# Statistics ahead of fused tile 0, one residual tile on VectorE, and a new order of tails and turnings in the middle passes of a hybrid layer

## What is computed

```python
x = x + attn(layernorm(x))        # itself normalised again, causal attention, plus its residual
x = x + ffn(layernorm(x))
x = x + s4d(layernorm(x))         # a long convolution over the first axis (here length 2), plus D * x
x = x + ffn(layernorm(x))

def ffn(x):                        # 256 -> 768 -> 256, weights rounded to fp8
    gate = silu((x @ fp8(gate_w)) * gate_scale)
    up   = (x @ fp8(up_w)) * up_scale
    return ((gate * up) @ fp8(down_w)) * down_scale
```

## Time and profile before

| what | value |
|---|---|
| median of 3 runs | 130.63 us (130.6 to 130.78) |
| the profiled execution | 130.82 us |
| its span, first to last instruction | 129.0 us |
| busy, share of the span: PE / DVE / POOL / ACT | 90% / 75% / 68% / 60% |
| granted TensorE clock | 1.000 |
| chain that ended last, by engine | PE 53%, DVE 26%, POOL 9%, issue 5%, DMA 2%, ACT 2% |
| pass 0 / 1 / 2 / 3 starts at | 54.6 / 71.94 / 89.53 / 107.83 us |

### The profile page before, as it was taken

One profiled execution on the slowest core, in us unless ns is written; L12 is line 12 of the kernel. 1 busy time (PEld: TensorE's weight loads), 2 busy tenths in 40 slices (PEclk: granted clock), 3 DMA queues, 4 the chain that ended last, 5 costly groups with the idle time before them and its releaser, 6 DMA issues.

```text
span 129.0 us, 2086 instructions
## 1 busy us (share of the span) xinstructions
PE 116.4 (90%) x666; PEld 77.1 (60%) x666; DVE 96.1 (75%) x224; ACT 77.3 (60%) x146; POOL 87.9 (68%) x172
## 2 busy tenths in 40 slices
PE   5997979977999999999999999989999879999930
PEld 5885548536767858746559545557446456455720
DVE  0499999999965587758675899947899944956471
ACT  2235368627966466957955368865578774486700
POOL 2256899999999888983333578889978860049631
PEclk9999999999999999999999999999999999999999
DMA  3999900000000000000000000000000000002204
GB/s 95 304 315 365 329 28 3 5 0 0 0 3 0 3 5 0 0 0 0 0 0 5 0 0 0 0 3 5 0 0 3 0 0 5 0 0 81 81 0 163
DMA packets 5666, 5.80 MB, mean 45 GB/s; under 512 B 1124, under 2 KB 5144, under 8 KB 5656
## 3 DMA queue, kind: packets, MB, share of 16 engines
q1 hardware_dynamic: 4776, 5.65, 13.1%
q10 hardware_dynamic: 816, 0.02, 0.4%
q0 software_dynamic: 64, 0.02, 0.1%
HBM read 4.63 MB, written 1.05 MB: 44 GB/s over the span
## 4 chain that ended last, share of the span: by engine, by line
PE 53%; DVE 26%; POOL 9%; issue 5%; DMA 2%; ACT 2%; POOLq 0%; DVEq 0%; ACTq 0%
PE psum L1170 21%; PE psum L1185 11%; PE psum L1109 7%; PE psum L1084 5%; POOL rstd L283 4%; DVE stats L680 4%; DVE down_raw L769 3%; DVE grid L760 3%; PE psum L1049 3%; PE psum L1131 2%; DMA x_in<-in_x 2%; DVE grid L761 2%; PE psum L1097 2%; POOL f_tail L439 2%; ACT h_rows L547 2%
## 5 line engine op out<-in xcount | busy, mean ns | idle before, releaser
L439 POOL TENSOR_TENSOR f_tail<-fused,f_head 128x512 f16<-128x512 f32 x12 | 14.3, 1189 | 15.7 <-ACT f_head L600 15.6
L595 ACT ACTIVATE gated<-psum,scales 128x512 f32<-128x512 f32 x24 | 16.4, 682 | 13.4 <-PE psum L1170 13.3
L1185 PE MATMUL psum<-down,f_head 128*128 128x256 bf16 x96 | 22.0, 273 | 0.5 <-POOL f_tail L439 0.5
L932 DVE SCALAR_TENSOR_TENSOR fused<-psum,up_scales_fit,gated 128x512 f32<-128x512 f32 x24 | 17.6, 738 | 5.9 <-PE psum L1170 3.6
L1185 PE MATMUL psum<-down,f_tail 128*128 128x256 bf16 x96 | 22.0, 272 | 0.0
L600 ACT ACTIVATE f_head<-fused 128x512 f16<-128x512 f32 x24 | 14.9, 621 | 2.5 <-DVE fused L932 2.4
L939 DVE TENSOR_TENSOR f_tail<-fused,f_head 128x512 f16<-128x512 f32 x12 | 8.7, 727 | 10.3 <-ACT f_head L600 10.3
L283 POOL TENSOR_TENSOR rstd<-var_eps,neg_half 128x2 f32<-128x2 f32 x16 | 13.1, 820 | 2.4
L1170 PE MATMUL psum<-h_head,up 128*128 128x512 f16 x48 | 14.3, 379 | 0.0
L1170 PE MATMUL psum<-h_tail,up 128*128 128x512 f16 x48 | 14.3, 379 | 0.0
L1170 PE MATMUL psum<-h_tail,gate 128*128 128x512 f16 x48 | 14.3, 379 | 0.0
(11 more groups left out here) (167 smaller groups left out, 260.0 us busy)
## 6 DMA issues: line engine op xcount, KB each, us to landing
x_in<-in_x SPq DMA_DIRECT2D x4, 256.0 KB, 4.5
out<-x_in SPq DMA_DIRECT2D x4, 256.0 KB, 2.1
qkv_sb<-in_qkv SPq DMA_DIRECT2D x3, 256.0 KB, 4.3
gate_raw<-in_gate_w SPq DMA_DIRECT2D x1, 768.0 KB, 6.4
up_raw<-in_up_w SPq DMA_DIRECT2D x1, 768.0 KB, 8.2
down_raw<-in_down_w SPq DMA_DIRECT2D x1, 768.0 KB, 9.9
wo_sb<-in_o_proj SPq DMA_DIRECT2D x1, 256.0 KB, 5.3
down_scale_all<-in_down_scale SPq DMA_DIRECT2D x1, 128.0 KB, 9.8
```

The lines of the kernel that those rows point to most:

```text
L439: pool.tensor_tensor(f_tail[:, m, :], fused[:, m % FUSED, :], f_head[:, m, :], ALU.subtract).then_inc(f_tail_by_pool, 1)
L595: act.activation(gated[:, m % 2, :], psum[:, BANK_GATE[m % 2], :], ACT.Silu, scale=gate_scales[:, m:m + 1]).then_inc(gated_ready, 1)
L932: dve.scalar_tensor_tensor(out=fused[:, m % FUSED, :], in0=psum[:, BANK_UP[m % 2], :], scalar=up_scales_fit[:, m:m + 1], in1=gated[:, m % ...
L1185: last = pe.matmul(column(BANK_DOWN[t // 2], H * (t % 2), H), part[:, m, t * P:t * P + P], down16[:, m, :], start=(m == 0 and t % 2 == 0 a ...
```

## The change

Six edits, all by hand in the engines' programs; the number of instructions on VectorE and GpSimd shifts by one each middle pass.

- VectorE: the last residual tile of the batch (x2 of tile 3 of 4) is added on VectorE (add_x1) instead of GpSimd, with its own semaphore; statistics of the first pair come before fuse(n, 0), those of the second pair after it; tail 0 stands between fuse 1 and fuse 2; tail 4 replaces tail 3 and stands behind fuse 5.
- GpSimd: three residual tiles instead of four; tails 1, 2, 3 in middle passes instead of 1, 2, 4, all in front of the last inversion; the shift is written ahead of the std product.
- ScalarE: the first pair of z rows stands before head 1.
- TensorE: on tile 0 of every pass the order is gate heads, up heads, gate tails, up tails; turn_h(n+1, 1) comes after down 4 instead of before it.

```diff
-        POOL_TAILS = [(1, 3, 4), (1, 2, 4), (1, 2, 4), (1, 3, 4)]
+        POOL_TAILS = [(1, 3, 4), (1, 2, 3), (1, 2, 3), (1, 3, 4)]
...
                 pool.wait_ge(rstd_ready[n], k + count)
+                pool.tensor_tensor(neg_mean_rstd[:, n, k:k + count], mean_rstd[:, n, k:k + count],
+                                   rstd[:, n, k:k + count], ALU.mult).then_inc(shift_ready[n], count)
                 if with_std:
                     pool.tensor_tensor(std[:, k:k + count], var_eps[:, n, k:k + count], rstd[:, n, k:k + count],
                                        ALU.mult).then_inc(std_ready, count)
-                pool.tensor_tensor(neg_mean_rstd[:, n, k:k + count], mean_rstd[:, n, k:k + count],
-                                   rstd[:, n, k:k + count], ALU.mult).then_inc(shift_ready[n], count)
...
-                    residual(0, x2, x1, range(first, first + T), x2_ready)
+                    residual(0, x2, x1, range(first, first + T - 1), x2_by_pool)
                     inverse_std(2, first, 2, negative_mean=True, with_std=True)
                     inverse_std(2, first + 2, 2, negative_mean=True, with_std=True)
                     tail(n, POOL_TAILS[n][0])
+                    tail(n, POOL_TAILS[n][1])
                     inverse_std(3, first, 2, negative_mean=True)
-                    tail(n, POOL_TAILS[n][1])
+                    tail(n, POOL_TAILS[n][2])
                     inverse_std(3, first + 2, 2, negative_mean=True)
-                    tail(n, POOL_TAILS[n][2])
...
                 gate(n, 2)
+                if n in (1, 2):
+                    z_rows(tiles[0])
+                    z_rows(tiles[1])
                 head(n, 1)
...
-                if n in (1, 2):
-                    z_rows(tiles[0])
-                    z_rows(tiles[1])
...
-                dve.wait_ge(x2_ready, tiles[-1] + 1)
+                b, t = tile_of[tiles[-1]]
+                dve.wait_ge(x2_by_pool, (T - 1) * b + min(t + 1, T - 1))
+                if t == T - 1:
+                    dve.wait_ge(x2_by_dve, b + 1)
                 tile_stats(2, tiles, x2)
+
+            def add_x1(k):
+
+                dve.wait_ge(down_read, k + 1)
+                dve.tensor_tensor(x2[:, k, :], scaled_down[:, k, :], x1[:, k, :], ALU.add).then_inc(x2_by_dve, 1)
...
+                    add_x1(tiles[-1])
+                    x2_stats(first)
                     fuse(n, 0)
-                    x2_stats(first)
                     x2_stats(second)
                     fuse(n, 1)
+                    tail(n, 0)
                     fuse(n, 2)
-                    tail(n, 0)
...
                     fuse(n, 4)
-                    tail(n, 3)
                     fuse(n, 5)
+                    tail(n, 4)
                     tail(n, 5)
...
             def gate_up(n, m):
-                for w, banks, made, read in ((gate16, BANK_GATE, gate_made, gated_ready), (up16, BANK_UP, up_made, fused_ready)):
+                if m == 0:
+                    for w, banks, made, read in BOTH:
+                        gate_up_part(n, m, w, banks, h_head, h_head_ready)
+                    for w, banks, made, read in BOTH:
+                        gate_up_part(n, m, w, banks, h_tail, h_tail_ready).then_inc(made, 1)
+                    return
...
                 turn_h(n + 1, 0)
                 down(n, M - 3)
+                down(n, M - 2)
                 turn_h(n + 1, 1)
-                down(n, M - 2)
                 down(n, M - 1)
```

More of the change, by code:

```diff
@@ L182, in hybrid_layer @@
         down_made, down_read = sem("down_made"), sem("down_read")
-        x2_ready, x3_ready, lag_ready, x4_by_pool, x4_by_dve = sem("x2_ready"), sem("x3_ready"), sem("lag_ready"), sem("x4_by_pool"), sem("x4_by_dve")
+        x2_by_pool, x2_by_dve, x3_ready, lag_ready, x4_by_pool, x4_by_dve = sem("x2_by_pool"), sem("x2_by_dve"), sem("x3_ready"), sem("lag_ready"), sem("x4_by_pool"), sem("x4_by_dve")
         tanh_in, tanh_out, trig_in, trig_out, magnitude_ready, taps_ready = sem("tanh_in"), sem("tanh_out"), sem("trig_in"), sem("trig_out"), sem("magnitude_ready"), sem("taps_ready")
-        POOL_TAILS = [(1, 3, 4), (1, 2, 4), (1, 2, 4), (1, 3, 4)]
+        POOL_TAILS = [(1, 3, 4), (1, 2, 3), (1, 2, 3), (1, 3, 4)]
         DVE_TAILS = [tuple(m for m in range(M) if m not in tiles) for tiles in POOL_TAILS]
@@ L1160, in _, with gate_up_part @@
             pe.wait_ge(gate_up_ready, 2)
-            def gate_up(n, m):
-                for w, banks, made, read in ((gate16, BANK_GATE, gate_made, gated_ready), (up16, BANK_UP, up_made, fused_ready)):
+            BOTH = ((gate16, BANK_GATE, gate_made, gated_ready), (up16, BANK_UP, up_made, fused_ready))
+            def gate_up_part(n, m, w, banks, part, ready):
+                for c in range(C):
+                    if m == 0 and w is gate16:
+                        pe.wait_ge(ready, n * C + (c + 1))
+                    last = pe.matmul(column(banks[m % 2], 0, S), w[:, c, m * P:m * P + P], part[:, c, :],
+                                     start=(part is h_head and c == 0), stop=(part is h_tail and c == C - 1))
+                return last
+            def gate_up(n, m):
+                if m == 0:
[4 more added lines that the diff above has]
+                    return
+                for w, banks, made, read in BOTH:
                     if m >= 2:
                         pe.wait_ge(read, n * M + (m - 1))
[L1166 to L1172, removed]
+                    gate_up_part(n, m, w, banks, h_head, h_head_ready)
+                    gate_up_part(n, m, w, banks, h_tail, h_tail_ready).then_inc(made, 1)
             def down(n, m):
```

## The result

The changed kernel takes 133.88 us (median of 4 runs, 133.8 to 133.9) against 130.7 us beside it (130.6 to 131.06): a ratio of 1.0237, 95% interval 1.0216 to 1.0257. It is slower by 3.2 us. The profiled execution took 133.9 us.

A forecast was written before the change was run, and what follows sets the result against it. GpSimd's closed chain was taken to set the middle passes, with TensorE 90% busy. Passes + 1.72 and + 0.24 us, last pass and start + 0.1, together + 2.1 on the median 130.63: 132.7; range 131.2 to 134.3.

The forecast's parts named there:

- the sum: Pass 1 + 1.72 us, pass 2 + 0.24, last pass and start + 0.1; together + 2.1, giving 132.7.
- S: Start of GpSimd's first inversion after its pass starts: 4.17 us in pass 1, 3.40 in pass 2; before, 3.78.
- The addition: VectorE's new residual addition ahead of the statistics: 0.38 us plus 0.22 for running beside a GpSimd addition.
- the rule of the Trainium skill: VectorE instructions with two SBUF inputs and GpSimd instructions reading SBUF exclude each other; the sum would be 0.2 to 0.4 longer.
- the row at 116.90: A VectorE tail before the change, 0.91 us where an undisturbed one took 0.69; source of the 0.22 disturbance.
- The chain: GpSimd from first inversion to end of last shift in a middle pass: 11.84 us, before 10.40 in pass 1.
- From the shift to the next pass: End of GpSimd's last shift to the next pass's start: 3.30 us instead of 3.41, through the moved turning.
- Idle time before up tile 2: TensorE in pass 1 waits 0.5 us more for fused tile 0, at no cost because the turning waits for GpSimd.
- Last pass: Last pass and start get 0 to 0.2 us longer, taken as 0.1.
- A sign that did not come: TensorE would be idle before the second turning for over 1 us in each middle pass.
- tail 4 in place of tail 3: On VectorE behind gated 5, it ends before the turning can start: cost 0.
- rival 1: ScalarE's late heads delay GpSimd's chain: 1.2 us of waits over both passes, with pass 2's old disturbances 134.0; chance 0.10.

The follow-up runs named there:

- e3: Kernel before with only the tails changed: GpSimd makes tails 1, 2, 3, all ahead of the last inversion, VectorE makes tail 4; ratio 1.0205.
- e4: Changed kernel with the second turning ahead of down tile 4 again; ratio 1.0173 to the kernel before.
- e5: Kernel before with only the first pair's statistics put ahead of fused tile 0 in both middle passes; ratio 1.0077.
- e10: Changed kernel with VectorE's fused tile 2 behind the first pair's convolution in pass 2; ratio 1.0207 to the kernel before.
- e7: Changed kernel with tails and second turning as before, and in pass 2 VectorE's fused tile 2 behind the first pair's convolution; ratio 0.9990 to the kernel before.

## Why the prediction was right, and where its size was off

The direction and the mechanism were right: slower, by GpSimd's third tail ahead of the last inversion, with 133.88 us inside the range of 131.2 to 134.3. The most likely value, 132.7, was 1.2 us low: the sum had + 1.72 and + 0.24 for the two passes, and they measured + 2.34 and + 0.80. Step by step:

- **S**, the first inversion after the start of its pass: forecast 4.17 and 3.40, measured 76.06 - 71.89 = 4.17 and 95.22 - 91.82 = 3.40. The 0.87 by which the late turning moves VectorE's beginning, the 0.67 won by fused tile 0, and the early scaled_down of pass 2 were right. The addition took 0.75 where I had 0.60. That fits VectorE waiting for GpSimd's second residual tile to end and GpSimd's third then waiting for the addition (it took 0.91 where the others took 0.73), as the rule of the Trainium skill that I had weighed has it, and not as the row at 116.90 had it; S did not suffer, because the addition started 0.06 sooner than I had it (74.27) and the statistics start a little ahead of the end that the record gives it.
- **The chain**: forecast 11.84, measured 12.22 and 12.38. This is the term that failed most, 0.38 and 0.54. The third tail (1.24) is as forecast, and e3, which has it alone, has a chain longer by 1.48 and 1.28. Mis-sized were the two inversions of norm 2 (80.39 - 76.06 = 4.33 and 99.55 - 95.22 = 4.33, forecast 4.03), because mean_rstd and the shift, and no longer the power, now fall beside VectorE's operations with two SBUF operands (0.60 and 0.46 where they take 0.20 alone): + 0.30 in each pass. From tail 1's start to tail 2's it took 1.62 in both passes (forecast 1.45), with a wait for head 2 of 0.46 in pass 1, and one of 0.28 behind a tail of 1.34 in pass 2: + 0.17. One more tail beside VectorE's operations took 1.33 (82.01) and 1.34 (104.14) instead of 1.16, and was 0.17 and 0.24 longer up to the next operation. Against this the first inversion of norm 3 took 1.67 and 1.73 up to its tail, where I had 1.89.
- **From the shift to the next pass**: forecast 3.30, measured 91.82 - 88.28 = 3.54 and 110.92 - 107.60 = 3.32. In pass 1 VectorE's tail 5 took 0.93 instead of 0.69, beside GpSimd's lag products, and down tile 5, which the moved turning had put right behind it, waited 0.83. Before, the same tail beside the same products took 0.69, so it is a matter of how the two fall together.
- **Idle time before up tile 2**: forecast 0.5 under GpSimd's. The record has 0.24 of idle time, but the start at 76.66 is 0.4 later than it would be at the pace of its neighbours, so the size was about right, and it lies under GpSimd's as forecast.
- **Last pass**: forecast 0.1, measured 0.0 within what the windows show.
- **A sign that did not come.** I had TensorE idle before the second turning for over 1 us in each pass. It is idle for 0.13 there (89.45, 108.79), because down tile 4, now in front of the turning, waits for VectorE's tail 4 (0.43 and 0.72) and the first turning waits too (0.82 and 0.39). That tail 4 in place of tail 3 costs nothing held by less than 0.1 us: h_rows are ready just after down tile 4 ends. In e4, where the turning stands ahead of down tile 4 again, it waits 1.60 and 1.90.
- **The rivals.** The measured time is 0.1 us from rival 1's 134.0 and 1.2 from the forecast's 132.7, but not by rival 1's mechanism. Of rival 1 (134.0) the waits for heads came true in part: 0.46 in pass 1 and 0.28 in pass 2, against the 1.2 us that it took, and the sum already had 0.4 of them. That the last shift would not wait for VectorE's second statistics held in pass 1. In pass 2 the margin was small: GpSimd's inversion at 105.62 stands 0.1 us behind VectorE's statistics, which the additions of 1.75 us had delayed. I had read the row of two additions (0.76) only as a price, and not asked which GpSimd operation would stand beside it when the engines move by a few tenths of a microsecond. e5 shows what that is worth by itself: 1.19 us in pass 2. In the changed kernel it is mostly hidden beside the third tail; e10 gives 0.3 us of the 0.56 that I was short there.
- **The Trainium skill's rule**, as I had priced it, would have made the sum 133.0 or so. That is nearer by luck: it put its 0.2 into S, and S came out at 4.17 without it. What the sum lacked lies in the chain and behind the last shift, in meetings of the same kind that I had not priced by the rule.

What stays open: that the inversions in the changed kernel meet VectorE at mean_rstd in both passes was read from the rows and not varied; what turns the order of the small operation and the addition was read from the rows too; and a version with the early z rows, the early shift and the early convolution in pass 2 but nothing else of the change was not run.

## What to carry to other kernels

Where an engine's row of work is closed from the operation that releases it to the one that others wait for, each operation moved in front of that last one costs its whole length (1.28 and 1.48 us of chain for a tail of 1.24 here): count them first, whatever else a change does. Where two engines exclude each other on some operations, an earlier start is not a gain by itself; look up which operation of the other engine will then stand beside each of them: here 0.3 us between two starts, and before them a few hundredths between a small operation and an addition, lay between the kernels with the long addition and those without. And two delays of one stage that lay on different engines did not add here, so that neither showed its size when it was taken away alone.

## What the runs showed of the hardware

Two VectorE additions of 128x256 with both operands in SBUF take 0.76 us together when GpSimd's tail (128x512, reading SBUF) starts 0.44 us behind the first, and 1.75 when it starts 0.13 behind it; the tail took 1.34 both times instead of the 1.16 that it took in e7, where it started behind both. The rows fit this reading: in the first case the tail waits for the second addition, which had begun about 0.1 us before it; in the other the first addition delays the tail, and the tail then holds back the second addition until it ends. I had priced such meetings at 0.2 us a time. The small GpSimd operations on 128x2 suffer too: 0.46 to 0.60 for 0.20 when a VectorE operation of that kind is under way.
